# Late conversion of four experts' weights, and a shorter token count, in a fused attention and mixture-of-experts kernel

## The chip, the cores and the metric

The kernel runs on one core of one Trainium2 chip. The metric is device microseconds (us) for one execution. The kernel before has a median of 637.37 us over 3 runs (630.87 to 637.79).

## What is computed

The reference, cut to what matters:

```python
x = x + tanh(g_xattn) * xattn(ctx, layernorm(x))   # top-30% mask of a 512x512 score matrix, for 4 batches
xf = layernorm(x).reshape(2048, 512)
yg = xf @ shared_gw.T; y, g = split(yg, 2)
shared = silu(g) * y @ shared_dw.T                 # 704 hidden columns
scores = sigmoid(xf @ gate_w.T)                    # 8 experts
_, topk_idx = top_k(scores + gate_bias, 2)
w = take_along_axis(scores, topk_idx); w = w / sum(w)
for e in range(8):                                 # up_w[e]: 704x512, down_w[e]: 512x352
    h = silu(xf @ up_w[e, :352].T) * (xf @ up_w[e, 352:].T)
    out = out + h @ down_w[e].T * we[:, None]      # we is 0 where e was not chosen
x = x + tanh(g_ffn) * (shared + out)
```

## The kernel before, in words

**Precision.** Products that need more than float16 are made of two float16 parts, a high and a low one, in three matmuls. So each weight is cut in two as well. One weight *item* is the up and down weights of one expert, or of one half of the shared network: items 0 and 1 are the shared halves, items 2 to 9 the experts 0 to 7. An item is cut into 8 *pieces* of 128x544 float32 (272 KB). A piece goes through a ring of 4 buffers (`stage`): SP's queue loads it (L280), ACT writes the high part (`high_piece`, L582) and, for most pieces, scales the staged copy in place (L586), and then either POOL (L482) or DVE (`low_piece`, L1068) subtracts to get the low part. Only then is the ring buffer free for the piece four later. `by_dve` tells which engine does the low part; DVE needs no scaled copy, so ACT has one pass instead of two.

**Stages.** (1) Attention of batch 0. (2) A loop over batches, in which the shared network of batch b runs beside the attention of batch b+1. (3) The last batch's shared network, beside the router and the building of the tables. (4) 39 expert tiles of 128 slots. Items 0 to 5 are converted in stages 1 and 2. Items 7 to 9 live in memory that stages 1 and 2 use for attention, so they come later.

**Stage 3 before.** PE runs six pieces of the shared up product (`shared_up`, L847, 24 matmuls each) and four down tiles (`shared_down`, L864, 18 matmuls each). DVE runs the router: `choose` (the two best experts of each token), `count_tokens` (L1313 to L1337: a prefix sum over 16 tiles by doubling, then one over 8 experts), `place` (slot number of each token), eight `hot_slots` steps (L1381 to L1386), which build one-hot matrices that PE multiplies (`slots`, L927) into the table of row indices and gate weights, and `table` (L1391, L1392). Between them it runs `shared_hidden` (L1224), on which the next up piece waits. There are two buffers for one-hot matrices, so step n waits for PE's step n-2. PE's order is fixed in the code: steps 0 to 4 stand among the last two up pieces, steps 5 to 7 among the first down tile. In the same stage items 6, 7 and 8 (24 pieces) are converted, four pieces to an up piece, and item 9 behind `table_ok`; the low parts go to POOL, three in four of the pieces, and to DVE. POOL then issues four gathers of rows (`gather`, L533). The first two go to buffers of their own, the next two into ring buffers, and so wait for the last conversions. PE waits for all items before the first expert tile (L966 to L968).

**Stage 4.** A tile t goes up (L981, L982: 48 matmuls), `silu` (ACT L744), `hidden` (DVE L1434), high and low part (ACT L749, DVE L1440), transposes (PE L991), a copy (DVE L1445), down (L1001: 9 matmuls), `expert_rows` (ACT L754), and a scatter with addition (`add_rows`, POOL L538). PE's order in a step is down(t), transposes of the gathered tile t+3 (L806), first half of up(t+2), transposes of hidden t+1, second half of up(t+2). POOL's order in a step is gather t+4, wait until add t-1 has landed, add t. `rows` has two buffers; `expert_rows(t)` waits until add t-2 has landed. The last part of stage 3, before the tiles, is `gathered_turned(0)` (DVE L1450), which waits for the last shared down tile because its target `x_t` shares memory with the shared hidden values.

Of the kernel before, what the change touches and what calls it, by code (L numbers as in the profile page):

```python
# [3 lines left out]
BATCHES, SEQ, C, D = 4, 512, 512, 128  # L4
# [17 lines left out]
PER_STEP = 4  # L22
# [4 lines left out]
EARLY = 7  # L27
CHUNKS = 8
# [18 lines left out]
def build(nc, x, ctx_t, wq_t, wk_t, gates, gate_wt, gate_bias, weights, out, xn_rows):  # L47
# [12 lines left out]
    with ExitStack() as ctx:  # L60
# [43 lines left out]
        work = sb("work", [P, 2 * KC * P + 2 * HP + 2 * HP + 2 * C + 2 * H])  # L104
        used = [0]

        def work_buf(words):
# [6 lines left out]
        x_t = work_buf(2 * KC * P).bitcast(F16).rearrange("p (s a c) -> p s a c", s=2, a=2 * KC)  # L114
# [3 lines left out]
        assert used[0] >= UPS * SEQ  # L118
        xg = work_buf(2 * C).bitcast(F16).rearrange("p (a c) -> p a c", a=2)
        xg_slots = [xg[:, 0, :], xg[:, 1, :]] + [stage[:, n, 0:C].bitcast(F16) for n in range(GATHERS - 2)]  # L120
# [7 lines left out]
        first = sb("first", [P, EXPERTS])  # L128
        warm = sb("warm", [P, 1])
# [16 lines left out]
        r = [sb(f"r{n}", [P, TILES, EXPERTS], F16 if n == 2 else F32) for n in range(6)]  # L146
# [11 lines left out]
        hot_cols = [hot[:, n * hot_words:n * hot_words + SLOTS_STEP * P].rearrange("p (a c) -> p a c", a=SLOTS_STEP) for n in range(2)]  # L158
        hot_vals = [hot[:, n * hot_words + SLOTS_STEP * P:(n + 1) * hot_words].rearrange("p (a v c) -> p a v c", a=SLOTS_STEP, v=2)
                    for n in range(2)]  # L160
# [69 lines left out]
        def by_dve(item, n):  # L230
            if not isinstance(item, int):
                return False
            if item == ITEMS - 1:
                return n % 2 == 1
            return n % RING == RING - 1 and (item >= EARLY - 1 or item * CHUNKS + n < BY_DVE)

# [37 lines left out]
        def _(sp):  # L274
# [121 lines left out]
        def _(pool):  # L396
# [9 lines left out]
            c.mark(pool.memset(tri[:], 0.0))  # L406
            c.mark(pool.memset(half_pow[:, 0, :], 0.5))
# [6 lines left out]
            for m in (ident, ident16):  # L414
# [4 lines left out]
                                      pattern=[[-1, P]], channel_multiplier=1))  # L419
            c.wait()  # L420
# [103 lines left out]
            for u in range(UPS):  # L524
                for n in range(u * PER_STEP, (u + 1) * PER_STEP):
                    if n % PER_STEP == PER_STEP // 2:
                        shared_low(BATCHES - 1, u)
                    low_piece(EARLY - 1 + n // CHUNKS, n % CHUNKS)
# [41 lines left out]
        def _(act):  # L570
# [146 lines left out]

            after(act, x1_st, TILES * 16)
            after(act, xn_st, TILES * 16)
            after(act, xt_mm, TILES)  # L720
            for u in range(UPS):
                if u == 0:
                    router_exp()
                shared_silu(BATCHES - 1, u)
                for n in range(u * PER_STEP, (u + 1) * PER_STEP):
                    if n - u * PER_STEP == PER_STEP // 2:
                        shared_high(BATCHES - 1, u)
# [788 lines left out]
```

## Time and profile before

| | us |
|---|---|
| median of 3 runs | 637.37 |
| profiled execution, device time | 635.86 |
| its span, first to last instruction | 634.1 |
| PE busy | 516.1 (81%) |
| DVE busy | 382.4 (60%) |
| ACT busy | 283.1 (45%) |
| POOL busy | 263.2 (42%) |

The profiled execution lies 1.5 us below the median; 1.8 us of it lie outside the span. Times in the rows below are us from the start of the span. Matmul ends are modelled, so consecutive starts are a better measure of PE's pace than the durations. A busy time of a merged row runs from its first start to its last end.

### The profile page before, as it was taken

The numbers are of one execution on the slowest core, as the hardware profiler recorded it, in microseconds if no ns is written. First come the engines' busy times: TensorE is split into PE (matmuls) and PEld (weight loads), VectorE is DVE, ScalarE is ACT, GpSimd is POOL, SyncE is SP. The second block draws the span as 40 slices with busy tenths as digits, with TensorE's granted clock in tenths as the row PEclk, the third lists the DMA queues.
The fourth block names the chain that finished last, engine by engine and source line by source line (L and its number), as shares of the span: only waits on it lengthen the run. The fifth ranks groups of instructions, "written<-read, shape, count | busy, mean of one in ns | idle before, by whom it ended". The sixth has DMA issues, their size and how long they took to land.

```text
span 634.1 us, 11448 instructions
## 1 busy us (share of the span) xinstructions
PE 516.1 (81%) x3139; PEld 290.1 (46%) x3140; DVE 382.4 (60%) x875; ACT 283.1 (45%) x511; POOL 263.2 (42%) x278
## 2 busy tenths in 40 slices
PE   2301588879996999779876979999999999999990
PEld 0100343434442454344344546666666666666650
DVE  0689758987898799977999343333333333333330
ACT  1696587736684568635664322222222222222220
POOL 1325834362444443451575333434343434343421
PEclk9855769979997999897888889999999999999996
DMA  4124383105610471045444533444444444444432
GB/s 133 63 70 146 101 282 110 54 18 176 233 44 18 142 260 53 19 165 174 125 137 142 165 106 68 76 91 75 90 74 91 79 87 78 88 75 91 74 43 33
DMA packets 33199, 65.79 MB, mean 104 GB/s; under 512 B 4176, under 2 KB 4432, under 8 KB 33168
## 3 DMA queue, kind: packets, MB, share of 16 engines
q1 hardware_dynamic: 23856, 43.88, 21.5%
q0 software_dynamic: 8736, 20.45, 18.2%
q10 hardware_dynamic: 576, 1.11, 0.6%
q8 instruction: 12, 0.20, 0.1%
q14 instruction: 19, 0.16, 0.1%
HBM read 42.10 MB, written 23.33 MB: 103 GB/s over the span
## 4 chain that ended last, share of the span: by engine, by line
PE 46%; DVE 33%; issue 7%; ACT 5%; DMA 4%; POOL 2%; SPq 1%; DVEq 1%; POOLq 0%; ACTq 0%
PE py L1001 12%; PE pg L981 11%; PE pu L982 11%; PE pt_bank L806 3%; DVE w L1100 3%; PE pu L864 2%; DVE w L1106 2%; DVE w L1171 2%; DVE w L1127 2%; PE pa L991 2%; DVE w L1123 2%; ACT w L621 2%; DVE w L1132 1%; DVE w L1116 1%; DVE w L1178 1%
## 5 line engine op out<-in xcount | busy, mean ns | idle before, releaser
L981 PE MATMUL pg<-w,work 128*128 x468 | 141.8, 315 | 3.4 <-DVE work L1450 3.4
L982 PE MATMUL pu<-w,work 128*128 x468 | 141.7, 315 | 0.0
L538 POOL DMA_INDIRECT out<-rows,idx x39 | 61.8, 1584 | 143.2 <-ACT rows L754 139.2
L482 POOL TENSOR_TENSOR w<-stage,w 128x544 f16<-128x544 f32 (+1 forms) x65 | 80.8, 1253 | 60.1 <-ACT stage L586 57.9
L847 PE MATMUL pg<-w 128*128 128x512 f16 (+1 forms) x288 | 82.0, 395 | 7.1 <-DVE work L1224 7.0
L744 ACT ACTIVATE work<-pg 128x352 f32<-128x352 f32 x39 | 18.1, 464 | 146.0 <-PE pu L982 146.0
L1001 PE MATMUL py<-w,work 128*128 x351 | 82.1, 379 | 0.8 <-DVE work L1445 0.8
L847 PE MATMUL pu<-w 128*128 128x512 f16 (+1 forms) x288 | 80.9, 391 | 0.0
L582 ACT ACTIVATE w<-stage 128x544 f16<-128x544 f32 (+1 forms) x80 | 51.5, 646 | 33.6 <-DMA stage<-in_weights 22.8
L1434 DVE SCALAR_TENSOR_TENSOR work<-pu,work 128x352 f32<-128x352 f32 x39 | 20.5, 525 | 73.6 <-ACT work L744 73.6
L981 PEld LDWEIGHTS pg<-w,work 128*128 128x128 f16 x468 | 46.1, 98 | 24.6 <-issue 4.3
L1445 DVE COPY work<-pa 128x768 f16<-128x768 f16 x39 | 21.8, 558 | 57.1 <-PE pa L991 57.1
L488 POOL TENSOR_TENSOR work<-work 128x512 f16<-128x512 f32 (+1 forms) x24 | 28.9, 1205 | 65.7 <-ACT work L651 65.4
L982 PEld LDWEIGHTS pu<-w,work 128*128 128x128 f16 x468 | 46.0, 98 | 20.6
L1001 PEld LDWEIGHTS py<-w,work 128*128 128x128 f16 x351 | 34.3, 98 | 37.2 <-issue 1.3
L847 PEld LDWEIGHTS pg<-w 128*128 128x128 f16 (+1 forms) x288 | 30.5, 110 | 41.5 <-DVE work L1224 10.8
L847 PEld LDWEIGHTS pu<-w 128*128 128x128 f16 (+1 forms) x288 | 31.5, 109 | 34.0 <-issue 4.2
L586 ACT ACTIVATE stage<-stage 128x544 f32<-128x544 f32 x65 | 42.7, 657 | 2.1
L793 PE MATMUL pa<-one,missed 128*1 128x1 f32 x8 | 0.8, 163 | 52.1 <-DVEq L1144 52.1
L864 PE MATMUL pu<-w,work 128*128 128x512 f16 (+1 forms) x144 | 41.5, 445 | 0.0
L621 ACT ACTIVATE w<-w 128x512 f16<-128x512 f32 x40 | 28.5, 715 | 26.0 <-DVEq L1098 26.0
L1440 DVE TENSOR_TENSOR work<-work 128x352 f16<-128x352 f32 x39 | 20.5, 526 | 28.1 <-ACT work L749 28.1
(203 smaller groups left out, 856.9 us busy)
## 6 DMA issues: line engine op xcount, KB each, us to landing
stage<-in_weights SPq DMA_DIRECT2D x76, 272.0 KB, 2.9
out<-rows SPq DMA_DIRECT2D x17, 256.0 KB, 3.9
w<-in_x SPq DMA_DIRECT2D x4, 1024.0 KB, 6.5
out<-w SPq DMA_DIRECT2D x16, 256.0 KB, 3.1
xn_rows<-w SPq DMA_DIRECT2D x16, 256.0 KB, 4.9
rows<-out SPq DMA_DIRECT2D x16, 256.0 KB, 3.0
stage<-in_weights ACTq DMA_DIRECT2D x4, 272.0 KB, 4.8
w<-in_ctx_t SPq DMA_DIRECT2D x4, 256.0 KB, 3.5
```

What stands on the lines that cost most here:

```text
L482: pool.tensor_tensor(w[:, ds(item, 1), 1, n * CHUNK_W:(n + 1) * CHUNK_W], stage[:, n % RING:n % RING + 1, :], w[:, ds(item, 1), 0, n * CHU ...
L488: pool.tensor_tensor(hid_tb[0:m, u, 1, :], hb[0:m, u % 2, :], hid_tb[0:m, u, 0, :], ALU.subtract).then_inc(hlo_sb, 1)
L538: pool.indirect_dma_start(out=out, out_offset=bass.IndirectOffsetOnAxis(ap=idx[:, t:t + 1], axis=0), in_=rows[:, t % 2, :], in_offset=None ...
L582: act.activation(w[:, ds(item, 1), 0, n * CHUNK_W:(n + 1) * CHUNK_W], stage[:, n % RING:n % RING + 1, :], ACT.Copy, scale=W_SCALE).then_in ...
L586: act.activation(stage[:, n % RING, :], stage[:, n % RING, :], ACT.Copy, scale=W_SCALE).then_inc(w_scaled, 1)
L621: act.activation(junk[:, i, :], sim[:, i, :], ACT.Sign, bias=cur[:, 0, i:i + 1], scale=-1.0, accum_out=acc[:, i - TPB // 2:i - TPB // 2 + ...
L847: mm = pe.matmul(bank_[0:m, :], w[:, half, part, at:at + m], x_tb[:, xpart * KC + k, :], start=(k, part, xpart) == (0, 0, 0), stop=(k, par ...
L864: mm = pe.matmul(bank_[:, :], hid_tb[0:m, u, part, i * P:(i + 1) * P], w[0:m, half, wpart, at:at + C], start=(u, part, wpart) == (0, 0, 0) ...
L981: pe.matmul(pg[p][:, 0:H], lhs, w[:, item, half, at:at + H], start=begin, stop=end)
L982: mm = pe.matmul(pu[p][:, 0:H], lhs, w[:, item, half, at + H:at + 2 * H], start=begin, stop=end)
L1001: mm = pe.matmul(py[:, :], hid_t[:, p, part * JC + j, :], w[:, item, half, at:at + C], start=(j, part, half) == (0, 0, 0), stop=(j, part) ...
L1445: dve.tensor_copy(hid_t[:, p, :, :], hid_banks[p]).then_inc(ht_sb, 1)
```

## The change

1. **Weights.** In stage 3 only item 6 and the first half of item 7 are converted (12 pieces), and behind the shared network and the table instead of among it. The other 20 pieces (second half of item 7, items 8 and 9) are converted in expert tiles 0 to 4, four to a tile, two on each side of `hidden_high` on ACT and of `hidden_low` ... `hidden_turned` on DVE. All low parts from item 6 on go to DVE; POOL has none. The first five tiles are written out for this on ACT and DVE, eight steps on PE. PE waits for 7 items before tile 0, for 8, 9 and 10 before tiles 5, 6 and 7. So that tile t never needs an expert above t, each expert gets at least one tile.
2. **Token count.** PE makes the sums over tiles by 32 small matmuls (`ranks`), and the prefix over experts becomes a product with a constant matrix (`lower`) and a reduction. The doubling copies and adds go.
3. **One-hot buffers.** Six instead of two. PE runs `slots` 0 to 4 behind the last up piece, the last three behind the first down tile.
4. **Homes.** `x_t` and all gather buffers no longer share memory with the ring or with the hidden values, so all four gathers go right behind the table, and `gathered_turned(0)` waits for no down tile. The memory for descriptors of POOL's DMAs is set to 8192 (`dynamic_dma_scratch_size`) instead of being left at its default.

```diff
+LATE = 6
+LATE_FIRST = 12
+LATE_TILES = 5
+PER_TILE = 4
-        x_t = work_buf(2 * KC * P).bitcast(F16).rearrange("p (s a c) -> p s a c", s=2, a=2 * KC)
-        xg_slots = [xg[:, 0, :], xg[:, 1, :]] + [stage[:, n, 0:C].bitcast(F16) for n in range(GATHERS - 2)]
+        xg = sb("xg", [P, 2, 2 * C], F16)
+        xg_slots = [hb[:, n, :].bitcast(F16) for n in range(2)] + [xg[:, n, :] for n in range(2)]
+        x_t = sb("x_t", [P, 2, 2 * KC, P], F16)
...
-            if item == ITEMS - 1:
-                return n % 2 == 1
+            if item >= LATE:
+                return True
...
 # SP
-            load_item(EARLY - 1)
-            after(sp, x1_st, TILES * 16)
-            after(sp, xn_st, TILES * 16)
-            after(sp, xt_mm, TILES)
-            load_item(EARLY)
-            load_item(EARLY + 1)
-            for n in range(RING):
-                load_piece(ITEMS - 1, n)
+            load_item(LATE)
             store_shared(tile0, 0)
             reload(BATCHES - 1, tile0, 2)
+            for n in range(RING):
+                load_piece(LATE + 1, n)
             store_shared(tile0, 1)
             reload(BATCHES - 1, tile0, 3)
+            for n in range(RING, CHUNKS):
+                load_piece(LATE + 1, n)
             store_shared(tile0, 2)
             store_shared(tile0, 3)
+            for item in range(LATE + 2, ITEMS):
+                load_item(item)
...
 # POOL
-            gather(0)
-            gather(1)
-            for n in range(CHUNKS):
-                low_piece(ITEMS - 1, n)
-            for t in range(2, GATHERS):
-                after(pool, w_lo[t - 2], ITEMS * (CHUNKS // RING))
+            for t in range(GATHERS):
                 gather(t)
...
 # ACT
+            for t in range(LATE_TILES):
+                silu(t, t % 2)
+                for piece in late_pieces(t)[:PER_TILE // 2]:
+                    high_piece(*piece)
+                hidden_high(t, t % 2)
+                if t == 1:
+                    for s in sh_st:
+                        after(act, s, TILES // 2 * 16)
+                if t:
+                    expert_rows(t - 1, (t - 1) % 2)
+                for piece in late_pieces(t)[PER_TILE // 2:]:
+                    high_piece(*piece)
...
 # PE
-                pe.matmul(pa[0][:, 0:P], tri[:], sel, start=True, stop=True).then_inc(route_mm, 1)
-                pe.matmul(pa[1][:, 0:P], ones[:], sel, start=True, stop=True).then_inc(route_mm, 1)
+                for t in range(TILES):
+                    mm = pe.matmul(pa[1][:, 0:EXPERTS], ones[:], sel[:, t, :], start=t == 0, stop=t == TILES - 1)
+                mm.then_inc(route_mm, 1)
+                for t in range(TILES - 1):
+                    later = TILES - 1 - t
+                    pe.matmul(pa[0][:, (t + 1) * EXPERTS:P].rearrange("p (t e) -> p t e", e=EXPERTS), ones[:],
+                              sel[:, t:t + 1, :].to_broadcast([P, later, EXPERTS]), start=t == 0, stop=False, skip_group_check=True)
+                mm = pe.matmul(pa[0][:, 0:P], tri[:], sel[:].rearrange("p t e -> p (t e)"), start=False, stop=True,
+                               skip_group_check=True)
+                mm.then_inc(route_mm, 1)
...
+            for step in range(SLOTS_STEPS - 3):
+                slots(step)
+            shared_down(BATCHES - 1, 0)
+            for step in range(SLOTS_STEPS - 3, SLOTS_STEPS):
+                slots(step)
...
-            for s in w_lo:
-                after(pe, s, ITEMS * (CHUNKS // RING))
-            after(pe, w_hi, ITEMS * CHUNKS)
+            weights_ready(LATE + 1)
...
+                    if late and LATE < t0 + k + 2 + HALVES < ITEMS:
+                        weights_ready(t0 + k + 2 + HALVES + 1)
...
 # DVE, count_tokens and what follows the table
-                o.then(dve.tensor_copy(total, pa[1][:, 0:P].rearrange("p (t e) -> p t e", t=TILES)))
-                while step < TILES:
-                    o.mark(dve.tensor_copy(c2[:, 0:step, :], a[:, 0:step, :]))
-                    o.then(dve.tensor_tensor(c2[:, step:, :], a[:, step:, :], a[:, :TILES - step, :], ALU.add))
+                o.then(dve.tensor_scalar(re8[:, 0, :], pa[1][:, 0:EXPERTS], float(P - 1), None, ALU.add))
+                o.then(dve.tensor_scalar(re8[:, 0, :], re8[:, 0, :], 1.0, None, ALU.max))
+                o.then(dve.tensor_tensor(before, lower[:], re8[:, 0, :].unsqueeze(1).to_broadcast([P, EXPERTS, EXPERTS]), ALU.mult))
+                o.then(dve.tensor_reduce(re8[:, 2, :], before, AX.X, ALU.add))
...
             table()
-            for i in range(TPB - 1):
-                shared_rows(BATCHES - 1, i)
-                for n in ((1, 3), (5,), (7,))[i]:
-                    low_piece(ITEMS - 1, n)
+            for n in range(RING):
+                low_piece(LATE, n)
+            shared_rows(BATCHES - 1, 0)
+            for n in range(RING, CHUNKS):
+                low_piece(LATE, n)
+            shared_rows(BATCHES - 1, 1)
+            for n in range(LATE_FIRST - CHUNKS):
+                if n == (LATE_FIRST - CHUNKS) // 2:
+                    shared_rows(BATCHES - 1, 2)
+                low_piece(LATE + 1, n)
...
-            after(dve, down_mm, TILES)
             gathered_turned(0, 0, 0)
...
+            for t in range(LATE_TILES):
+                hidden(t, t % 2)
+                for piece in late_pieces(t)[:PER_TILE // 2]:
+                    low_piece(*piece)
+                hidden_low(t, t % 2)
+                gathered_turned(t + 2, t % 2, t + 1)
+                hidden_turned(t, t % 2)
+                for piece in late_pieces(t)[PER_TILE // 2:]:
+                    low_piece(*piece)
...
-    nc = bacc.Bacc("TRN2", target_bir_lowering=False, num_devices=1)
+    nc = bacc.Bacc("TRN2", target_bir_lowering=False, num_devices=1, dynamic_dma_scratch_size=8192)
```

## Rows read from the trace of the kernel before

**Rows 1.** Busy time by stretch: start:end, length, engines, PEclk, DMA share, GB/s

```profile
287.50:369.40 81.90, 65.80 (x315) 34.82 (x311) 65.72 (x127) 43.67 (x72) 39.55 (x32) 0.88 0.48 146
388.00:394.30 6.30, 6.30 (x50) 4.01 (x49) 2.27 (x4) 1.65 (x3) 2.58 (x2) 1.00 0.45 79
```

**Rows 2.** Chain that ended last, 298 to 363: start, length, what

```profile
298.43 0.65 PE pu L847 x3
299.87 1.14 DVE r L1318
...
347.37 3.84 PE pu L864 x9
...
358.69 4.11 DMA stage<-in_weights
```

**Rows 3.** Waits, 288 to 370: who for whom, total, times, longest

```profile
PE pa L927 <- DVE w L1386: 9.4, 5, 3.0
```

**Rows 4.** Timeline of PE in stage 3: start, length, line, operation

```profile
286.87 0.83 PE L831 MATMUL pt_bank<-gw,w 128*128 128x16 f16 x24
...
306.15 0.81 PE L847 MATMUL pu<-w 128*96 128x512 f16 x3
309.66 0.82 PE L847 MATMUL pg<-w 128*128 128x512 f16 x3 [2.70 <-DVE work L1224]
...
351.00 2.36 PE L927 MATMUL pa<-w 128*128 128x78 f32 x16
353.20 4.05 PE L864 MATMUL py<-w,work 128*128 128x512 f16 x18
...
369.38 0.47 PE L981 MATMUL pg<-w,work 128*128 x1 [3.45 <-DVE work L1450]
```

**Rows 5.** Timeline of DVE in stage 3

```profile
321.77 1.33 DVE L1385 TENSOR_TENSOR w<-w,slot_f 128x156 f32<-128x156 f32 x1
...
335.35 0.32 DVE L1385 TENSOR_TENSOR w<-w,slot_f 128x156 f32<-128x156 f32 x1
...
353.40 0.26 DVE L1391 TENSOR_SCALAR idx<-pa,iota_p 128x39 int32<-128x39 f32 x1 [3.85 <-PE pa L927]
```

**Rows 6.** The low part on DVE, all 15: minimum/median/maximum ns

```profile
L1068 DVE SCALAR_TENSOR_TENSOR w<-stage,w x15: 710/726/2797, 44.8 to 366.7; 128x544 f16<-128x544 f32 x15
```

**Rows 7.** Timeline of POOL in stage 3

```profile
321.65 2.53 POOL L482 TENSOR_TENSOR w<-stage,w 128x544 f16<-128x544 f32 x2 [0.82 <-ACT stage L586]
...
356.42 0.99 POOL L533 DMA_INDIRECT work<-xn_rows,idx  x1 [0.30 <-ACT w L582]
```

**Rows 8.** Timeline of one expert tile: ACT, DVE, POOL, PE

```profile
392.57 0.46 ACT L744 ACTIVATE work<-pg 128x352 f32<-128x352 f32 x1 [3.65 <-PE pu L982]
394.60 0.69 ACT L754 ACTIVATE rows<-py,w_slot 128x512 f32<-128x512 f32 x1 [0.33 <-PE py L1001]
...
394.39 0.53 DVE L1440 TENSOR_TENSOR work<-work 128x352 f16<-128x352 f32 x1 [0.73 <-ACT work L749]
397.09 0.56 DVE L1445 COPY work<-pa 128x768 f16<-128x768 f16 x1 [1.52 <-PE pa L991]
...
389.77 1.59 POOL L538 DMA_INDIRECT out<-rows,idx  x1 [3.72 <-ACT rows L754]
396.13 1.56 POOL L538 DMA_INDIRECT out<-rows,idx  x1 [3.48 <-ACT rows L754]
...
396.47 0.50 PE L991 MATMUL pa<-ident,work 128*128 128x128 f16 x6
```

**Rows 9.** DMA issues: names, queue, count, KB each, median us to landing

```profile
stage<-in_weights SPq DMA_DIRECT2D x76, 272.0 KB, 2.9
out<-rows SPq DMA_DIRECT2D x17, 256.0 KB, 3.9
...
stage<-in_weights ACTq DMA_DIRECT2D x4, 272.0 KB, 4.8
...
out<-rows,idx POOLq DMA_INDIRECT x39, 4.7
```

More of the change, by code:

```diff
@@ L21 @@
 BY_DVE = 20
-PER_STEP = 4
 KEEP = int(SEQ * 0.3)
@@ L128, in build @@
         first = sb("first", [P, EXPERTS])
+        lower = sb("lower", [P, EXPERTS, EXPERTS])
         warm = sb("warm", [P, 1])
@@ L145, in build @@
         lg = sb("lg", [P, TILES, 2, EXPERTS])
-        r = [sb(f"r{n}", [P, TILES, EXPERTS], F16 if n == 2 else F32) for n in range(6)]
+        r = [m.rearrange("p (t e) -> p t e", t=TILES) for m in (wq_s, wk_s)]
+        r += [sb(f"r{n}", [P, TILES, EXPERTS], F16 if n == 2 else F32) for n in range(2, 6)]
         rc = sb("rc", [P, 7, TILES])
@@ L406, in _ @@
             c.mark(pool.memset(tri[:], 0.0))
+            c.mark(pool.memset(lower[:], 0.0))
             c.mark(pool.memset(half_pow[:, 0, :], 0.5))
@@ L419, in _ @@
                                       pattern=[[-1, P]], channel_multiplier=1))
+            c.mark(pool.affine_select(out=lower[:], in_=lower[:], compare_op=ALU.is_ge, fill=float(P), base=0,
+                                      pattern=[[-1, EXPERTS], [1, EXPERTS]], channel_multiplier=0))
             c.wait()
@@ L524, in _ @@
             for u in range(UPS):
[L525 to L528, printed above, removed]
+                shared_low(BATCHES - 1, u)
             def gather(t):
@@ L716, in _ @@
             keep_logits(BATCHES - 1)
+            router_exp()
+            for u in range(UPS):
+                shared_silu(BATCHES - 1, u)
+                if u:
+                    shared_high(BATCHES - 1, u - 1)
+            shared_high(BATCHES - 1, UPS - 1)
+            for n in range(CHUNKS):
+                high_piece(LATE, n)
+            act.wait_ge(table_ok, 1)
             after(act, x1_st, TILES * 16)
@@ L720, in _ @@
             after(act, xt_mm, TILES)
[L721 to L727, printed above, removed]
[L728 to L738 removed]
+            after(act, up_mm, BATCHES * UPS)
+            for n in range(LATE_FIRST - CHUNKS):
+                high_piece(LATE + 1, n)
             def silu(t, p):
@@ L754, in expert_rows @@
                 act.activation(rows[:, p, :], py[:, :], ACT.Copy, scale=w_slot[:, ds(t, 1)]).then_inc(y_sb, 1)
-            silu(0, 0)
-            hidden_high(0, 0)
-            for s in sh_st:
-                after(act, s, TILES // 2 * 16)
-            with act.Fori(0, SLOT_TILES // 2) as i:
+            for t in range(LATE_TILES):
[10 more added lines that the diff above has]
+                    high_piece(*piece)
+            with act.Fori(LATE_TILES // 2, SLOT_TILES // 2) as i:
                 for k in range(2):
@@ L963, in _, with weights_ready @@
             shared_down(BATCHES - 1, TPB - 1)
-            for s in w_lo:
-                after(pe, s, ITEMS * (CHUNKS // RING))
-            after(pe, w_hi, ITEMS * CHUNKS)
+            def weights_ready(items):
+                for s in w_lo:
+                    after(pe, s, items * (CHUNKS // RING))
+                after(pe, w_hi, items * CHUNKS)
+            weights_ready(LATE + 1)
             def up(t, p, item, ks):
@@ L1018, in _, with expert_steps @@
             turn_and_up(1, 1, item_of(1))
-            def expert_steps(t0, n0, steps, turn=True):
+            def expert_steps(t0, n0, steps, turn=True, late=False):
                 down_item = item_of(t0)
@@ L1034, in _ @@
             assert loops * GATHERS == SLOT_TILES - 3
-            with pe.Fori(0, loops) as i:
+            for i in range(2):
+                expert_steps(i * GATHERS, i, GATHERS, late=True)
+            with pe.Fori(2, loops) as i:
                 expert_steps(i * GATHERS, i, GATHERS)
```

108 lines of the change are left out of this document (35 added, 73 removed).

## The prediction

> **What bounds the kernel now.** I read the busy time by stretch first. In the expert tiles PE is busy for all of the 6.30 us of a tile, at a granted clock of 1.00 [rows 1]. So 39 tiles hold about 246 us in which nothing but less PE work can help, and the change takes no matmul out of them. The stretch before the first tile is another matter: 81.9 us, PE and DVE busy about 66 us each, granted clock 0.88 [rows 1]. That is where a gain can come from.
>
> Next, the chain of waits in that stretch. It leaves PE for DVE as early as 299.9 (the prefix copies), touches PE again when the slot matmuls and a down tile run at half pace (9 matmuls in 3.84 us), and comes to a DMA of weights at 358.69 [rows 2]. The waits agree: PE stood 9.4 us in five waits for DVE's one-hot matrices at `slots` [rows 3], and 3.45 us before the first tile [rows 4]. The reader should see two causes in series: the router's chain on DVE up to the table (353.4), and the last weights from there to 369.38 [rows 4, 5].
>
> Why is DVE slow? The same instruction, L1385, took 1.33 us at 321.77 and 0.32 us at 335.35 [rows 5]; the long one lies wholly within two low parts that POOL did from 321.65 to 324.18 [rows 7]. The prefix copy of 128x8 elements took 1.14 us [rows 2]. DVE waits until POOL's instruction ends. POOL does 22 low parts in this stretch at about 1.25 us each (2.53 for two [rows 7]); the change takes all of them away. Six `shared_low` stay.
>
> [...]
>
> **PE's floor after the change.** I follow PE in its new order, as it has the first say if DVE is quick. Up to the end of the third up piece nothing changes but `ranks`: the piece's last three matmuls start at 306.15 [rows 4] and three take 0.65 us [rows 2], so it ends at 306.8. `ranks` gets 30 more matmuls. The trace has none of their kind; below lie 24 of 16 columns in 0.83 us, 0.035 each [rows 4]; above the float32 slot matmuls, 16 in 2.2 us, 0.14 each [rows 4]. So 1.0 to 4.1 us; they are float16 and at most 120 columns wide, nearer the lower row; I take 1.5. That gives 308.3. Three more up pieces are 3 x 8 x 0.65 = 15.6: 323.9. Five slot steps at 1.1 (two took 2.2 [rows 4]) 5.5: 329.4. Down tile 0 is 18 matmuls, 3.9: 333.3. Three slot steps 3.3: 336.6. The table follows on DVE within 0.5: about 337.1, where it is 353.9 now (353.40 and two operations of 0.26). So the table comes 16.8 us earlier. Down tiles 1 and 2 take 7.8, the turned rows 0.9, down tile 3 3.9: 349.2. That is PE's floor for the first expert tile.
>
> **Is DVE in time for that?** A `hot_slots` step has four operations, some 1.5 us when nothing blocks (L1385 at 0.32 [rows 5], the others alike), up to 4 with POOL beside it. The count loses its doubling steps, four of which hung 1 us each on POOL, and is over by about 302, the placing by 305. Up piece u+2 then waits no longer for `shared_hidden(u)`; the first such wait cost PE 2.70 us before 309.66 [rows 4]. With six buffers, steps 0 to 5 are made while PE is still on the up pieces; steps 6 and 7 by 330, before 333.3. So the 9.4 us of [rows 3] go to nothing. What covers this is five up pieces of PE, 26 us, over some 20 us of DVE work behind `choose`. If that cover were gone, each us of DVE would be one of the table.
>
> **What then comes last: the ring.** The conversion of 12 pieces stands behind the table, and all of it stands before `gathered_turned(0)` on DVE, which up(0) waits for. Queued behind each low part are `shared_rows(1)`, then `shared_rows(2)`, for which down tile 3 and tile 0 on PE wait. Low parts are 0.65 apart (0.73 long [rows 6]). Pieces 0 to 3 of item 6 are loaded and made high already: low by 337.1 + 4 x 0.65 = 339.7. Piece 4 is loaded into the first buffer freed, at 337.8. A load lands in 2.9 us, or 4.8 when four are issued at once beside other traffic [rows 9]; the one on the chain took 4.11 [rows 2]. With 3.7, ACT 0.65 and DVE 0.73, piece 4 is low at 343, and piece 7, at 1.1 us a piece, at 346.2. Then `shared_rows(1)`: 347. Down tile 3 starts there (2 us of PE idle) and ends at 350.9. SP meanwhile has stored tile 0 of the rows at 340.4 and waits for it to land before its reload (3.9 us at most by the median [rows 9]): item 7's pieces are loaded from 344 on, the first is low at 349, the fourth at 352.5. `gathered_turned(0)` 0.7: up(0) at 353.2. Now it starts at 369.38 [rows 4]. Gain 16.2.
> With loads at 2.9 and no queueing this is 349.5, PE's floor: gain 20. With loads at 4.8 twice over and a DMA queue shared with four gathers: 357, gain 12.
>
> **The gathers and homes.** Gathers are 1.5 us apart (0.99 each and their issue [rows 7]), so four go from 338 to 343. The first two land before PE turns them at 344.4 only if they land within some 4 us. Late gathers cost nothing while down tile 3 waits anyway. POOL's waiting ends there.
>
> **Tiles 0 to 4.** Per tile ACT gets four passes of 0.65 = 2.6 us and DVE four of 0.7 = 2.9, beside 1.65 and 2.27 busy [rows 1]: 4.3 and 5.2 of 6.30. Order matters more. On ACT two high parts stand between `silu` (392.57) and `hidden_high`, on DVE two low parts ahead of `hidden_low`. This moves the end of `hidden_low` from 394.92 to about 395.6; PE transposes at 396.47 [rows 8]. Cover 0.9 us, hence nothing in tiles 1 to 4. The other two low parts follow the copy of 397.09 [rows 8] and end at 399.1, before the next `hidden` at 399.4. Loads have 3.3 us (second pair) to 4.9 us (first pair) from issue to use; 2.9 to 4.8 fits closely. In tile 0 there is no down tile between, and `hidden_low` is on the path: two passes more, 0.9. For late loads in tiles 1 to 5 I put another 0.9, between 0 and 5. Sum: +1.8.
>
> **POOL's adds.** An add lands 4.7 us after its issue [rows 9], and the next is issued 6.36 later [rows 8]; from landing to issue it needs about 0.8, so a tile has 0.8 us to spare. Beside the weights' loads adds will land later, but `expert_rows` waits only for the add before last, a whole tile of 6.3 us in reserve. Priced at nothing.
>
> **Sum.** Span 634.1 - 16.2 + 1.8 = 619.7; with the 1.8 outside the span 621.5. The profiled run lay 1.5 under the median; so the sum may be 1.5 short on a median, which is inside the range.
>
> **Rivals.**
> 1. *The stage ends on PE's floor* (all loads at 2.9): up(0) at 349.5, total 618 with the same tiles. With ranks at 1.0 and nothing lost in the tiles, 615. Chance 0.15.
> 2. *The late tiles stall.* [...] If the 2.9 us of low parts stood in the tile's chain in full, less 1.5 us between `hidden_low` and the transposes, five tiles would lose 1.4 each = 7: 628. For it: DVE's low part took up to 2.80 us beside POOL [rows 6]. Against: a gather is 0.99 and an add 1.6 us long, and most of an add falls on DVE's free time. Chance 0.15.
> 3. *Not faster.* The smaller descriptor memory makes POOL wait for free descriptors at each gather or add, in all 39 tiles. It decides once an add comes later by the spare 0.8 us: beyond it every us per tile is 39 in all. It cancels the gain of 14 at 0.8 + 14/39 = 1.2 us per tile; at 1.5 us the time is 621.5 + 27 = 649. For it: four gathers are out at once, and the trace shows nothing of descriptors in hand. Against: before the tiles run, at most four gathers and two adds are open. Chance 0.08.
> 4. *The ring eats the gain.* Each round of four pieces takes 5.5 us, so up(0) at 357: 625, and with a slow start of PE 627. Chance 0.12, partly in the forecast's own range.
>
> **How the numbers follow.** The forecast, 617 to 626, has 0.5; its figure is 621.5. Rivals 1, 2 and 4 (0.42) give 615 to 628, so 614 to 629 leaves out rival 3 and the tails of 2 and of the rest. A measurement of this kernel can tell about 1%, here 6.4 us, from no change. Faster by over 1% means under 631.0: all of forecast and rivals 1 and 4, most of 2: 0.88. Within 1%: the worst of 2 and a mild 3, 0.06. Slower: 0.06.
>
> **What would show it.** L1385 and its kin at 0.3 us in all but a few of eight steps; no wait of PE for DVE at `slots`; the table's first operation near 336.7; down tile 3 late by about 2 us behind `shared_rows(1)`; up(0) near 353, waiting for `gathered_turned(0)`; tiles of 6.30 us from tile 2 on. Wrong if the tiles of 0 to 7 are longer by over 1 us each, if POOL's adds follow each other at more than 6.4 us, or if PE waits at `ranks` or for down tile 0.

## The result and the profile after

The changed kernel takes 616.89 us (median of 4 runs, 616.15 to 618.4) against 636.42 us for the kernel before (4 runs): ratio 0.9706, 95% interval 0.9665 to 0.9747. The profiled executions are 635.86 us before and 616.15 after, 19.7 apart; their spans are 634.1 and 614.4.

Busy time by stretch of the changed kernel, in the columns of [rows 1]: the whole of the stretch that answers to the 81.9 us before, the part of it behind the table, and a tile with late weights.

```profile
287.80:354.30 66.50, 58.57 (x334) 31.73 (x331) 45.17 (x111) 17.16 (x29) 12.93 (x11) 0.96 0.30 95
334.00:354.00 20.00, 12.37 (x66) 5.42 (x64) 10.48 (x17) 5.25 (x8) 4.85 (x5) 0.99 0.69 211
377.00:383.30 6.30, 6.30 (x49) 4.00 (x47) 4.84 (x9) 3.94 (x7) 2.92 (x3) 1.00 1.00 263
```

DVE's busy time in the stretch has fallen from 65.7 to 45.2 us and POOL's from 39.6 to 12.9. The granted clock is 0.96 instead of 0.88. Between 293.3 and 321.0, where PE no longer stops among the up pieces, it is 1.00; the kernel before had stretches at 0.50 behind its stops, for example from 311.0 to 313.5 and from 347.5 to 351.0. The tile with late weights lasts 6.30 us as before, though the DMAs are busy all the time.

The timeline of PE after:

```profile
287.81 1.44 PE L853 MATMUL pg<-w 128*128 128x512 f16 x3
...
297.74 0.55 PE L928 MATMUL pa<-r,ones 128*128 128x8 f16 x16
298.14 0.64 PE L932 MATMUL pa<-r,ones 128*128 128x120 f16 x15
298.65 0.22 PE L934 MATMUL pa<-r,tri 128*128 128x128 f16 x1
...
322.01 4.59 PE L941 MATMUL pa<-w 128*128 128x78 f32 x40
326.43 4.05 PE L870 MATMUL pu<-w,work 128*128 128x512 f16 x18
330.32 2.80 PE L941 MATMUL pa<-w 128*128 128x78 f32 x24
...
344.83 4.07 PE L870 MATMUL py<-w,work 128*128 128x512 f16 x18 [0.79 <-DVE rows L1245]
354.33 0.47 PE L991 MATMUL pg<-w,x_t 128*128 x1 [5.44 <-DVE x_t L1447]
...
364.51 2.10 PE L1011 MATMUL py<-w,work 128*128 x9
...
602.09 2.11 PE L1011 MATMUL py<-w,work 128*128 x9 [0.75 <-DVE work L1442]
```

The rows of the kernel before that answer to the first, the next to last and the last of these:

```profile
288.49 1.44 PE L847 MATMUL pg<-w 128*128 128x512 f16 x3
...
379.25 2.11 PE L1001 MATMUL py<-w,work 128*128 x9
...
617.44 2.11 PE L1001 MATMUL py<-w,work 128*128 x9 [0.75 <-DVE work L1445]
```

The 9.4 us of [rows 3] are gone: the slot matmuls have no wait beside them. The table's first operation is at 333.16 (353.40 before), the first expert tile at 354.33 (369.38 before [rows 4]). In its place stands a new wait of 5.44 us, for DVE's turned rows. What lies behind that is the chain that ended last, a store of rows for which SP's queue waits and then a load into the ring:

```profile
322.17 4.42 PE pa L941 x40
326.59 3.89 PE pu L870 x18
330.49 2.65 PE pa L941 x24
...
334.37 1.99 DVE w L1082 x3
...
337.11 7.18 DMA out<-rows
...
345.29 4.82 DMA stage<-in_weights
...
364.67 1.94 PE py L1011 x9
```

Set out by stretches, the two profiled executions differ so (starts from the two traces; the last stretch is told below):

| stretch | before | after | gain |
|---|---|---|---|
| start to the last batch's first up piece | 288.49 | 287.81 | 0.7 |
| from there to the table | 64.9 | 45.4 | 19.6 |
| table to first expert tile | 16.0 | 21.2 | -5.2 |
| first tile to first down product | 9.9 | 10.2 | -0.3 |
| first to last down product (38 tiles) | 238.2 | 237.6 | 0.6 |
| last down product to the end | 16.7 | 12.3 | 4.4 |

So the first expert tile starts 15.1 us earlier where 16.2 were forecast, by a sum whose parts are off, and 4.4 us come from a place where the forecast had nothing. The second line is from one pair of executions, and of four traces whose code is that of the kernel before up to the table this pair has the longest: 64.9 us against 63.9, 61.6 and 61.6. The changed kernel has 45.4 here and 44.7 in a second trace. The experiments take the last line first, then the table's gain and the ring. Each was compared with the kernel before on its own chip; on those three chips the kernel before had medians of 636.18, 634.92 and 635.45 us.

### The profile page after: what moved, and what is told of

Its sections match the earlier page's. It is cut to its first block, busy times and chain, and to the rows that moved or that the text cites. A ratio compares the mean times of both kernels' runs of the same rounds, so it can differ in the third digit from the quotient of the medians.

```text
span 614.4 us, 11359 instructions
## 1 busy us (share of the span) xinstructions
PE 508.7 (83%) x3169; PEld 287.4 (47%) x3170; DVE 374.3 (61%) x880; ACT 268.4 (44%) x489; POOL 236.7 (39%) x258
## 4 chain that ended last, share of the span: by engine, by line
PE 52%; DVE 27%; issue 6%; DMA 6%; ACT 4%; POOL 2%; SPq 1%; DVEq 1%; POOLq 0%; ACTq 0%
PE py L1011 12%; PE pg L991 12%; PE pu L992 11%; PE pt_bank L812 3%; DVE w L1114 3%; PE pg L853 3%; PE pu L853 3%; PE pu L870 2%; DVE w L1120 2%; DVE w L1185 2%; DVE w L1141 2%; PE pa L1001 2%; DVE w L1137 2%; ACT w L625 2%; DVE w L1146 2%
## 5 line engine op out<-in xcount | busy, mean ns | idle before, releaser
L991 PE MATMUL pg<-w,x_t 128*128 x468 | 141.7, 314 | 5.4 <-DVE x_t L1447 5.4
L992 PE MATMUL pu<-w,x_t 128*128 x468 | 141.6, 314 | 0.0
L853 PE MATMUL pg<-w 128*128 128x512 f16 (+1 forms) x288 | 80.6, 390 | 3.5 <-DVE work L1238 3.4
L494 POOL TENSOR_TENSOR w<-stage,w 128x544 f16<-128x544 f32 (+1 forms) x43 | 53.4, 1252 | 31.1 <-ACT stage L590 29.2
L1431 DVE SCALAR_TENSOR_TENSOR work<-pu,work 128x352 f32<-128x352 f32 x39 | 20.5, 525 | 65.7 <-ACT work L742 65.7
L991 PEld LDWEIGHTS pg<-w,x_t 128*128 128x128 f16 x468 | 46.0, 98 | 26.6 <-issue 6.3
L992 PEld LDWEIGHTS pu<-w,x_t 128*128 128x128 f16 x468 | 46.0, 98 | 20.5
L870 PE MATMUL pu<-w,work 128*128 128x512 f16 (+1 forms) x144 | 37.9, 417 | 0.1
L1082 DVE SCALAR_TENSOR_TENSOR w<-stage,w 128x544 f16<-128x544 f32 x37 | 28.2, 792 | 11.9 <-ACT w L586 10.6
```

Of the source, the lines that this page charges most:

```text
L494: pool.tensor_tensor(w[:, ds(item, 1), 1, n * CHUNK_W:(n + 1) * CHUNK_W], stage[:, n % RING:n % RING + 1, :], w[:, ds(item, 1), 0, n * CHU ...
L853: mm = pe.matmul(bank_[0:m, :], w[:, half, part, at:at + m], x_tb[:, xpart * KC + k, :], start=(k, part, xpart) == (0, 0, 0), stop=(k, par ...
L870: mm = pe.matmul(bank_[:, :], hid_tb[0:m, u, part, i * P:(i + 1) * P], w[0:m, half, wpart, at:at + C], start=(u, part, wpart) == (0, 0, 0) ...
L991: pe.matmul(pg[p][:, 0:H], lhs, w[:, item, half, at:at + H], start=begin, stop=end)
L992: mm = pe.matmul(pu[p][:, 0:H], lhs, w[:, item, half, at + H:at + 2 * H], start=begin, stop=end)
L1082: dve.scalar_tensor_tensor(out=w[:, item, 1, n * CHUNK_W:(n + 1) * CHUNK_W], in0=stage[:, n % RING, :], scalar=W_SCALE, in1=w[:, item, 0, ...
```

## The experiments

**The kernel before, traced again.** No edit.

> The kernel before, unchanged, for a second trace. In the first trace 11.3 us lay between the start of the last add (622.82) and the end of the span, against 6.9 us in the changed kernel: 4.4 us of the difference of 19.7. Theory 'tail is chance': a second trace has about 7 us there and a span near 630, and the total is unclear by about 1%. Theory 'tail belongs to the kernel': again 11 us and 634 +- 1.

Median 636.92 us (10 runs), ratio 1.000 (0.9972 to 1.0029). The tail came back, 11.4 us: it belongs to the kernel. Timeline of POOL:

```profile
core 0 of [0], span 635.0 us
618.00 1.55 POOL L538 DMA_INDIRECT out<-rows,idx  x1 [4.25 <-ACT rows L754]
623.62 1.55 POOL L538 DMA_INDIRECT out<-rows,idx  x1 [4.08 <-DMA out<-rows,idx]
```

Its busy time by stretch splits those 11.4 us:

```profile
623.60:628.60 5.00, 0.00 (x0) 0.00 (x0) 0.00 (x0) 0.00 (x0) 1.55 (x1) 0.50 0.43 52
628.60:635.00 6.40, 0.00 (x0) 0.00 (x0) 0.00 (x0) 0.00 (x0) 0.00 (x0) 0.50 0.00 0
```

The last add lands within 5 us, and then 6.4 us pass in which no engine computes and no DMA moves a byte (0 GB/s).

**Only `dynamic_dma_scratch_size`.**

```diff
-    nc = bacc.Bacc("TRN2", target_bir_lowering=False, num_devices=1)
+    nc = bacc.Bacc("TRN2", target_bir_lowering=False, num_devices=1, dynamic_dma_scratch_size=8192)
```

> The kernel before with the memory for descriptors set to 8192, nothing else. Rival 3 (POOL waits for free descriptors): adds follow each other at more than 6.36 us, total up by 5 us or more. Theory that it is priced at nothing: adds 6.30 to 6.36 us apart, total within 0.3% of the kernel before. If the descriptor memory makes the tail: last add to end of span 6.9 us instead of 11.3, total 4.4 us less.

Median 631.8 us (10 runs), ratio 0.9931 (0.9901 to 0.996): 4.4 us faster. The same two stretches of its trace, whose span is 626.8:

```profile
620.20:625.20 5.00, 0.00 (x0) 0.00 (x0) 0.00 (x0) 0.00 (x0) 1.53 (x1) 0.52 0.40 52
625.20:626.80 1.60, 0.00 (x0) 0.00 (x0) 0.00 (x0) 0.00 (x0) 0.00 (x0) 0.50 0.00 0
```

The empty stretch at the end shrinks from 6.4 to 1.6 us; the add lands as before. Nothing is given back in the tiles (adds land in 4.7 us by the median, 5.0 at most, as before). That the option sets a memory for descriptors, and a smaller one than the default, is how the forecast reads it; the runs show the times. The span is 8.2 us shorter than that of the trace above, more than the medians differ: this execution, at 628.56 us, is the shortest of its ten. Of the 8.2 us 1.9 lie ahead of the first up piece and 2.2 between it and the table, which comes 61.6 us behind it, as it does in the next run with the option at its default. So the last line of the table is this option, and the third rival had the sign wrong.

**Only the last loads moved to SP's queue.** The edit takes ACT's only DMAs away, another thing that the change did.

```diff
             store_shared(tile0, 0)
             reload(BATCHES - 1, tile0, 2)
+            for n in range(RING, CHUNKS):
+                load_piece(ITEMS - 1, n)
...
-                act.dma_start(stage[:, n % RING, :], weights[ITEMS - 1, :, n * CHUNK_W:(n + 1) * CHUNK_W]).then_inc(w_ld[n % RING], 16)
```

> The kernel before with the last four weight pieces issued from SP's queue, behind the first store of rows, instead of from ACT's; so ACT issues no DMA at all, as in the changed kernel. If ACT's DMA queue makes the tail: last add to end of span about 7 us instead of 11.3. The loads land up to 2 us earlier, since SP waits only for the ring: first expert tile at 367 to 370. Total 632 to 636 if the tail is ACT's, 634 to 638 if not.

Median 634.75 us, ratio 0.9996 (0.9964 to 1.0028). The last add starts at 621.29 and the span ends at 632.6: 11.3 us again. ACT's queue is not the cause. The first tile starts at 367.91, within what was expected.

**POOL's low parts given back as idle work.** The changed kernel with 22 subtractions on POOL whose result nobody reads.

```diff
+            spare = [x_t.rearrange("p s a c -> p (s a c)").bitcast(F32), xg[:].rearrange("p s c -> p (s c)").bitcast(F32)]
+            o.then(pool.memset(spare[0], 0.0))
+            o.then(pool.memset(spare[1], 0.0))
             for u in range(UPS):
                 shared_low(BATCHES - 1, u)
+                for n in range(4 if u < 4 else 3):
+                    o.then(pool.tensor_tensor(spare[0][:, 0:CHUNK_W], spare[1][:, 0:CHUNK_W], spare[1][:, 0:CHUNK_W], ALU.subtract))
```

> The changed kernel with 22 subtractions of 128x544 float32 given back to POOL in stage 3, into memory that nobody reads, beside the router. It puts the cost on DVE back without any other part of the conversion. Theory 'POOL's low parts made DVE slow': operations with two inputs take up to 1.3 us again, DVE is 10 us longer on the same work, PE waits for it at the up pieces or the slots, and the table comes 5 to 10 us later, total 622 to 627. If PE's covering work (up pieces and slots one after the other) is enough: DVE slow, but table and total within 1 us of the changed kernel's 333 and 616.9.

Median 630.4 us, ratio 0.9898 (0.9863 to 0.9934): 13.5 us more than the changed kernel's 616.89 and 11.3 more than the 619.12 of its second measurement below, both from other chips; by the ratios it is 10 to 12 us. The total lies above the expected 622 to 627. The table comes at 346.72, 13.6 us later where 5 to 10 were expected, the first tile at 366.73, 12.4 later. Groups of DVE's work up to the first tile, first in the changed kernel, then here (columns: count, busy us, mean ns, idle before):

```profile
L1384 DVE TENSOR_TENSOR w<-w,slot_f 128x156 f32<-128x156 f32 x8 | 3.4, 431 | 0.0
L1385 DVE TENSOR_TENSOR w<-w,slot_f 128x156 f32<-128x156 f32 x8 | 3.4, 428 | 0.3
```

```profile
L1387 DVE TENSOR_TENSOR w<-iota_col,slot_f 128x512 f32<-128x512 f32 x8 | 11.1, 1388 | 0.0
...
L1389 DVE TENSOR_TENSOR w<-w,slot_f 128x156 f32<-128x156 f32 x8 | 7.9, 990 | 0.0
L1390 DVE TENSOR_TENSOR w<-w,slot_f 128x156 f32<-128x156 f32 x8 | 7.7, 957 | 0.3
```

The same two products have gone from 0.43 to 0.97 us by the mean. The waits of this kernel between 288 and 357 show how it reaches PE:

```profile
PE pg L858 <- DVE work L1243: 5.8, 2, 3.9
...
PE pa L946 <- DVE w L1390: 1.7, 1, 1.7
...
PE pu L875 <- POOL work L500: 1.6, 1, 1.6
```

That is 9.1 us of the 13.6; the rest is mostly matmuls at half pace behind two of the waits (granted clock 0.54 from 324.6 to 327.6 and 0.59 from 345.0 to 346.7), and a stage that began 0.9 us later. One part of it, 1.6 us, is POOL late with its own `shared_low`, which the idle work delays as well. So the removal of POOL's low parts carries most of what the stage gains. A measure that leaves the beginning of the stage out is the time from PE's first rank matmul to the table's first operation: 54.5, 54.6, 51.3 and 52.4 us in the four traces of the kernel before and its two variants, 47.6 here, and 35.4 in both traces of the changed kernel and in the five versions below that alter nothing ahead of the table. The idle work gives 12.2 of the 16 to 19 us back that lie between the two kernels. The forecast's cover, PE's up pieces over DVE's work, held in the changed kernel, where PE waits for DVE nowhere ahead of the table, and did not hold here, with 5.8 us of waits at the up pieces.

**The changed kernel again, as the measure of the next three.**

> The changed kernel unchanged, beside the variants of this call. First tile at 354 +- 1, last add to end of span 6.9 us, total 616 to 618.

Median 619.12 us (617.1 to 619.79), ratio 0.9737 (0.9684 to 0.979). First tile at 354.27, last add 6.8 us before the end of the span. The total is 1.1 us above what was expected. The adds landed in 6.8 us at most here, 5.6 in the first trace, with the same median of 4.8.

**The old token count.** Two matmuls for the ranks, doubling on DVE, all else as changed.

```diff
-                for t in range(TILES):
-                    mm = pe.matmul(pa[1][:, 0:EXPERTS], ones[:], sel[:, t, :], start=t == 0, stop=t == TILES - 1)
...
+                pe.matmul(pa[0][:, 0:P], tri[:], flat, start=True, stop=True).then_inc(route_mm, 1)
+                pe.matmul(pa[1][:, 0:P], ones[:], flat, start=True, stop=True).then_inc(route_mm, 1)
...
+                while step < TILES:
+                    o.mark(dve.tensor_copy(c2[:, 0:step, :], a[:, 0:step, :]))
+                    o.then(dve.tensor_tensor(c2[:, step:, :], a[:, step:, :], a[:, :TILES - step, :], ALU.add))
```

> The changed kernel with the old token count: two matmuls for the ranks, doubling copies and adds on DVE. DVE's count and placing grow by some 3 us, PE's ranks shrink by 0.9. If PE's up pieces cover DVE: total 616 +- 1, table at 332 to 333.5. If the count was on the path: table 2 to 3 us later, total 619 to 620.

Median 620.02 us (616.5 to 620.14), ratio 0.9729 (0.9669 to 0.9789): by total time not to be told from 0.9737. The trace is sharper. The table is at 336.63 against 333.98, though the stage began within 0.1 us of the other; PE's waits in this kernel from 297 to 330:

```profile
PE pg L853 <- DVE work L1231: 2.3, 1, 2.3
```

`shared_hidden(1)` stands behind count and placing, and the fourth up piece waits for it. But not all of the 2.6 us is the count's: PE left half pace later in this trace (granted clock from 293 to 294 0.50 against 1.00), and its first rank matmul came at 299.58 against 298.56.

```profile
299.58 0.22 PE L928 MATMUL pa<-r,tri 128*128 128x128 f16 x1
```

From there to the table it is 37.05 us against 35.42. So the shorter count is worth 1.6 us of the table's gain: the count was on the path, for somewhat less than the second expectation has.

**Two one-hot buffers,** with the old places of the steps.

```diff
-                     for home in (sim.rearrange("p i c -> p (i c)"), att.rearrange("p i c -> p (i c)"), hot) for n in range(2)]
+                     for home in (hot,) for n in range(2)]
...
+                elif u == UPS - 2:
+                    shared_up(BATCHES - 1, u, ks=range(0, KC // 2))
+                    slots(0)
+                    shared_up(BATCHES - 1, u, ks=range(KC // 2, KC))
```

> The changed kernel with two one-hot buffers and the old places of the one-hot steps on DVE and PE. If the buffers and the new order were worth much: PE waits 3 us or more for DVE at the slots and the table comes at 336 or later, total 620. If POOL's low parts alone made the waits at the slots: waits under 1 us, table within 1 us of 333, total 616 to 618.

Median 617.78 us, ratio 0.9725 (0.9668 to 0.9782). One wait of 0.94 us at the slots, the table at 334.50 with a stage that began 0.5 us earlier than in the changed kernel beside it: 1.0 us, which total time doesn't show. With POOL quiet, two buffers leave 0.94 us of the 9.4 of [rows 3], so POOL made most of these waits. With POOL busy and six buffers (the version with idle work) 1.7 us are left at the slots, but PE waits 5.8 among the up pieces instead. POOL's low parts, the count and the buffers, each taken alone, come to 12.2, 1.6 and 1.1 us; what the remaining 1 to 4 us of the 16 to 19 are was not tested.

**Eight pieces ahead of the tiles.**

```diff
-LATE_FIRST = 12
-LATE_TILES = 5
+LATE_FIRST = 8
+LATE_TILES = 7
...
             store_shared(tile0, 0)
             reload(BATCHES - 1, tile0, 2)
-            for n in range(RING):
-                load_piece(LATE + 1, n)
             store_shared(tile0, 1)
             reload(BATCHES - 1, tile0, 3)
-            for n in range(RING, CHUNKS):
-                load_piece(LATE + 1, n)
+            load_item(LATE + 1)
...
```

> The changed kernel with 8 instead of 12 pieces ahead of the first tile and 24 in tiles 0 to 5; SP does stores and reloads of rows first, then item 7. Theory 'the ring behind the table ends the stage' (12 pieces, DMA about full from 334 to 354): first tile at 348 to 350, total 611 to 613. Rival: the stores and reloads of the rows end it (store landed 7.2 us after issue): first tile at 353 or later, total as the changed kernel's. Rival: the late tiles have no room for a sixth: PE waits before tile 5 to 7, 2 us or more of the gain gone.

Median 614.18 us, ratio 0.9647 (0.9592 to 0.9702): 4.9 us below the changed kernel's 619.12 on this chip. The first tile starts at 351.04, 16.7 us behind the table instead of 20.3. That is less than expected, since down tile 3 still starts only at 345.85, behind the gathered rows. And the tiles give some 2 us back (from the first down product to the last add 246.5 us against 244.0 in the changed kernel beside it): SP issues the last two stores of rows behind eight loads, at 360.80, ACT waits for them, and the adds and gathers come late. The longest add took 7.4 us to land. Waits of this kernel from 352 to 396:

```profile
ACT rows L749 <- DMA out<-rows: 3.1, 1, 3.1
...
PEld pt_bank L809 <- DMA work<-xn_rows,idx: 2.3, 2, 1.6
```

**The loads of item 7 ahead of the reload.**

```diff
             store_shared(tile0, 0)
-            reload(BATCHES - 1, tile0, 2)
             for n in range(RING):
                 load_piece(LATE + 1, n)
+            reload(BATCHES - 1, tile0, 2)
             store_shared(tile0, 1)
```

> The changed kernel with SP issuing the four loads of item 7 ahead of the reload of the rows, which waits until the first store has landed (7.2 us). Theory 'SP blocked behind that store ends the stage': the first load of item 7 goes out at 339 to 341 instead of 344.8, first tile at 351 to 352, total 2 to 3 us less. Rival 'the DMAs are full from 334 to 354 anyway': loads go out earlier and land no earlier, first tile at 354 +- 1, total the same.

Median 613.93 us, ratio 0.9672 (0.9637 to 0.9707). SP's queue in the changed kernel, then here:

```profile
337.11 0.34 SPq L325 DMA_DIRECT2D out<-rows  x1
344.38 0.33 SPq L321 DMA_DIRECT2D rows<-out  x1
344.81 1.79 SPq L291 DMA_DIRECT2D stage<-in_weights  x4
```

```profile
337.17 0.34 SPq L325 DMA_DIRECT2D out<-rows  x1
338.83 5.40 SPq L291 DMA_DIRECT2D stage<-in_weights  x4
344.42 0.37 SPq L321 DMA_DIRECT2D rows<-out  x1
```

Four loads used to sit behind a reload that waits for a store to land. With the order turned, the first two go out 5 to 6 us earlier and the other two 2 to 3, and the first tile is 18.5 us behind the table (21.2 and 20.3 in the two traces of the changed kernel). PE waits 1.59 us before it instead of 5.44, and its first matmuls are at full pace (0.32 us instead of 0.47), so the first down product comes 8.9 us after the first tile's start instead of 10.2. By the medians the one line moved is worth 2 to 5 us (613.93 against 616.89 and 619.12 from other chips, and against 615.98 of the version with 4096 on this one); the intervals of the ratios overlap, so it is the trace that shows it. The rival, that the DMAs are full anyway, falls: the loads landed earlier, and the DMAs' busy share in the 20 us behind the table was 0.69.

**`dynamic_dma_scratch_size` at 4096** in the changed kernel.

> The changed kernel with 4096 instead of 8192 for POOL's descriptors. Theory 'the end of the program takes time by the size of that memory': 11.3 us after the start of the last add with the default, 6.9 with 8192, so 4.5 to 5 with 4096 and total 2 us less. Rival 3 of the forecast, now where it should bite: adds more than 6.4 us apart, total up by 10 us or more. Third: nothing changes.

Median 615.98 us, ratio 0.9696 (0.966 to 0.9733). The last add starts at 610.96, the span ends at 617.2: 6.2 us, where 8192 gave 6.5 to 6.9 and the default 11.3 to 11.4. Half the number took 0.3 to 0.7 us off the end, where the first step took 4.4 to 4.9. Adds do not get slower: 4.8 us by the median and 5.6 at most, as in the changed kernel's first trace. The total is the same within its interval.

**Put together.** Eight pieces, DVE's order, PE's order and SP's order changed as the last findings say:

```diff
             store_shared(tile0, 0)
-            reload(BATCHES - 1, tile0, 2)
...
             store_shared(tile0, 1)
+            reload(BATCHES - 1, tile0, 2)
             reload(BATCHES - 1, tile0, 3)
...
-            for i in range(1, TPB - 1):
+            for i in range(1, TPB):
                 shared_down(BATCHES - 1, i)
             after(pe, lg_sb, BATCHES)
             turn_gathered(0, 0, 0)
             turn_gathered(1, 1, 0, xt_second)
-            shared_down(BATCHES - 1, TPB - 1)
...
-            weights_ready(LATE + 1)
+            weights_ready(LATE)
...
             shared_rows(BATCHES - 1, 0)
-            for n in range(RING, CHUNKS):
-                low_piece(LATE, n)
             shared_rows(BATCHES - 1, 1)
+            for n in range(RING, CHUNKS - 2):
+                low_piece(LATE, n)
+            shared_rows(BATCHES - 1, 2)
...
             gathered_turned(1, 1, 0, xt_second)
+            for n in range(CHUNKS - 2, CHUNKS):
+                low_piece(LATE, n)
...
```

> A version put together from what was measured: 8 pieces ahead of the tiles and PE waiting for item 6 only before tile 4; DVE does rows 0 and 1 of the shared network before the low parts of pieces 4 to 7, of which two come behind the turned rows; PE does down tile 3 before it turns gathered rows; SP does two stores, two reloads, half of item 7, the last stores. First tile at 347 to 349, PE not waiting over 1 us between table and first tile, total 609 to 613. If loads then hit the first tiles, tiles 0 to 4 lose 2 us or more and the total is 613 to 616.

Median 611.72 us (610.59 to 612.86), ratio 0.9639 (0.9604 to 0.9675): the fastest, 23.7 us below the kernel before on its chip. It beats the changed kernel too, whose medians were 616.89 and 619.12 on other chips, and whose copy with 4096 took 615.98 on this one (615.21 to 618.98, clear of this version's four runs). First tile at 350.16, 15.4 us behind the table; 1.2 us later than expected, as PE waits 2.7 us for the turned rows. The tiles lose nothing: from the first down product to the last add it is 243.1 us, 243.0 in the changed kernel's first trace.

> The same with 4096 for POOL's descriptors: 2 us less than the version with 8192 if the end of the program scales with it, the same if not.

Median 612.25 us, ratio 0.9629 (0.9585 to 0.9674). The last add starts at 604.37 and the span ends at 610.3: 5.9 us against 6.55 with 8192. No difference in the total.

## Why the prediction was right, and where it was off

The forecast of 621.5 was 4.6 us above the median, and direction and size were right. The result lies within 614 to 629, but just under the 617 to 626 that had the chance of 0.5, between the 618 and the 615 that the first rival gave. That rival's mechanism did not happen: the stage did not end on PE's floor, as PE stood 5.44 us before the first tile. So the total alone would have pointed to the wrong story, and that the forecast came so near is in part luck, as the last point shows. Step by step:

- **DVE is slow because of POOL's low parts: right, and it carries most of the change.** The idle subtractions alone brought 10 to 13 us back. Held up were not only operations with two inputs (L1385 with 1.33 us instead of 0.32 [rows 5]) but also three of the doubling copies (the forecast has four), which have one. In the kernel before, the copies and POOL's instructions beside them:

```profile
299.87 1.14 DVE L1318 COPY r<-r 128x8 f32<-128x8 f32 x1
...
301.24 1.01 DVE L1318 COPY r<-r 128x16 f32<-128x16 f32 x1
...
302.46 1.08 DVE L1318 COPY r<-r 128x32 f32<-128x32 f32 x1
...
303.74 0.20 DVE L1318 COPY r<-r 128x64 f32<-128x64 f32 x1
```

```profile
298.54 2.45 POOL L482 TENSOR_TENSOR w<-stage,w 128x544 f16<-128x544 f32 x2 [16.73 <-ACT stage L586]
300.95 1.27 POOL L488 TENSOR_TENSOR work<-work 128x512 f16<-128x512 f32 x1
302.18 1.32 POOL L482 TENSOR_TENSOR w<-stage,w 128x544 f16<-128x544 f32 x1
```

Three copies ended 0.02 to 0.04 us behind an instruction of POOL (301.01 behind 300.99, 302.25 behind 302.22, 303.54 behind 303.50). The fourth and largest, with POOL idle from 303.50 to 304.08, took 0.20. What holds DVE up meanwhile no trace shows.
- **The table: 336.7 forecast, 333.16 measured.** Three terms were off, all to the same side. Slot steps 1.1 us each; measured 8 instructions, that is one step, in 0.88 (40 in 4.42). The row taken for it [rows 4] is from a moment when PE was just leaving half pace (granted clock 0.50 from 347.5 to 351.0 and 0.77 from there to 353.0), as the down tile ahead of it shows [rows 2]; that makes 1.7 us for eight steps. `ranks` 1.5 us, measured 0.96. And the half pace at the beginning cost some 0.5 us less (the first 18 matmuls of the stage took 6.04 us instead of 6.54), in a stage that began 0.7 us earlier.
- **The table behind DVE or behind PE: PE, as forecast,** with DVE idle for 4.99 us before the table's first operation. The up pieces cover DVE, but with the old count they did not (PE waited 2.3 us at one of them): the count's share is 1.6 us. The forecast had named its end time and not its price.
- **The ring ends the stage: right in kind, 4.7 us too small.** 16.5 us forecast from the table's first operation to the first tile, 21.2 measured. The term that failed is the store for which SP waits: priced at 3.9 us by a median of all such stores, it took 7.18, beside four gathers and four loads, and everything in SP's queue stood behind it. That is 3.3 of the 4.7; a load of 4.82 instead of some 3.7 is another 1.1. The new order of SP's queue took some of it back, which shows it. In size, behind the table, this is what the fourth rival had (its first tile at 357 is 20.3 us behind the table); the early table hid it.
- **The gathers cost nothing: not quite.** All four went right behind the table, at 334.66, 336.49, 337.76 and 339.01; in the kernel before the third started at 367.52. PE waited 1.2 us for the second gather and 0.8 for `shared_rows(1)`. Both lie ahead of down tile 3, where the ring is later still.
- **The late tiles: +1.8 forecast, nothing lost.** The first down product comes 0.3 us later behind the first tile's start, and the 38 tiles behind it take 0.6 us less. Tiles 1 to 4 run at 6.30 to 6.34 us, at DMA busy shares from 0.68 up to full. The second rival falls: in the five late tiles gathers took up to 1.34 us instead of 0.99 in one trace and 1.01 in the other, and adds landed in 5.6 and 6.8 us at most instead of 5.0, within POOL's and `rows`' reserve. Whether DVE's low parts lengthened them, or the loads did, was not tested. The margin is thin, though: the version with eight pieces shows a late store turning into 2 us of late tiles.
- **`dynamic_dma_scratch_size`, the forecast's descriptor memory: wrong in sign.** The third rival made it a loss of 0 to 27 us; alone it is a gain of 4.4 us, in a place that the forecast had put at nothing, the end of the program. The forecast's span of 619.7 was 5.3 us above the measured 614.4. This is 4.4 of them. The errors of the other steps nearly cancel, which is luck: -3.5 at the table, +4.7 at the ring, -2.1 in the tiles.

## What to carry to other kernels

Count POOL's subtractions at DVE's price as well, when both run in the same stretch: here 22 of them whose result nobody reads cost 10 to 13 us, mostly by what they did to DVE. When a queue holds a transfer that waits for another to land, put what is urgent ahead of it; the price of such a wait was the landing time in that crowd, 7.18 us, and not the median over the kernel, 3.9. And look at the end of the trace: what lies behind the last transfer may be set by a build option and not by any instruction, as the 6.4 us here that became 1.6.

## What the runs showed of the hardware

- From the last add's start to the end of the span it took 11.3 to 11.4 us in the three traces with `dynamic_dma_scratch_size` at its default, 6.5 to 6.9 in the nine with 8192, and 6.2 and 5.9 in the two with 4096. The kernel before was run with the default and 8192, the changed kernel and the last version with 8192 and 4096. Less the 4.7 us in which adds land by the median, an estimate of what lies behind the last landing is 6.6, 1.8 to 2.2, and 1.2 to 1.5 us. In the kernel before the stretch without any work shrank from 6.4 to 1.6 us. What is done in that time, and why it is not in proportion to the number, no trace shows.
- With 4096, POOL's 39 gathers and 39 adds ran as fast as with 8192: gathers took 0.99 us of POOL by the median in both, with the first four issued within 4.4 us, and adds landed in 4.8 us by the median in both, in 5.6 and 6.4 at most with 4096 and in 5.6 and 5.8 in the same two kernels with 8192, where a second trace of the changed kernel had 6.8.
- PE held 6.30 us a tile at a DMA busy share of 1.00 and 263 GB/s, which is more than three times the 79 GB/s of [rows 1].
- From PE's first rank matmul to the table the changed kernel and the five versions with nothing altered there take 35.42 or 35.43 us, in seven traces, and the version with idle work on POOL 47.57.
